# Routed pages of a mixture of experts: two accumulators in place of three, the first twelve pages asked for together, and the experts' splits moved by four pages

## What is computed

```python
x = hidden_states.reshape(-1, H)                  # 2048 tokens, H = 256
topk_w, topk_idx = top_k(softmax(x @ gate_w.T), 4)   # 4 of 16 experts a token
topk_w = topk_w / topk_w.sum(axis=-1, keepdims=True)
shared = (silu(gate) * up) @ shared_down.T        # width 704, every token
shared = shared * sigmoid(x @ shared_gate_vec.T)
for each expert e:                                # inner width 176
    h = silu(x @ w_gate[e].T) * (x @ w_up[e].T)
    acc = acc + (h @ w_down[e].T) * weight_of_e[:, None]
out = x + layernorm(shared + acc)
```

## Time and profile before

| | before |
|---|---|
| time, median of 3 runs | 621.13 us (619.58 to 626.93) |
| the profiled execution's own time | 622.44 us |
| its span, first to last instruction | 620.7 us |
| mean granted TensorE clock | 0.938 |
| instructions | 11606 |
| DMA | 86.34 MB, mean 139 GB/s |
| PE / DVE / ACT / POOL busy | 84 / 66 / 55 / 53% |

### The profile page before, as it was taken

One profiled execution on the slowest core, in us unless ns is written; L12 is line 12 of the kernel. 1 busy time (PEld: TensorE's weight loads), 2 busy tenths in 40 slices (PEclk: granted clock), 3 DMA queues, 4 the chain that ended last, 5 costly groups with the idle time before them and its releaser, 6 DMA issues.

```text
span 620.7 us, 11606 instructions
## 1 busy us (share of the span) xinstructions
PE 523.1 (84%) x3550; PEld 401.6 (65%) x3550; DVE 408.0 (66%) x1005; ACT 342.7 (55%) x701; POOL 325.9 (53%) x357
## 2 busy tenths in 40 slices
PE   2737899899999998878887886968999999999573
PEld 1624455656565453356666775857999999999452
DVE  6539878888788857249735644635997666665337
ACT  2241576696578558655442315535887666666314
POOL 5431543481464215215276566624778887777624
PEclk9859899999999999989897988987999999999878
DMA  7231661535063440340036323439998888887595
GB/s 271 74 129 52 194 192 46 168 128 155 21 216 104 132 136 2 101 141 2 9 138 214 119 81 123 164 125 256 230 248 164 147 150 141 138 134 108 68 343 199
DMA packets 71034, 86.34 MB, mean 139 GB/s; under 512 B 6272, under 2 KB 64192, under 8 KB 70976
## 3 DMA queue, kind: packets, MB, share of 16 engines
q1 hardware_dynamic: 53264, 63.15, 32.3%
q0 software_dynamic: 14448, 19.31, 18.0%
q10 hardware_dynamic: 3264, 3.15, 1.5%
HBM read 33.68 MB, written 39.12 MB: 117 GB/s over the span
## 4 chain that ended last, share of the span: by engine, by line
PE 35%; DVE 8%; issue 4%; DMA 3%; ACT 3%; another core or an unknown queue 2%; POOL 1%; ACTq 0%; POOLq 0%; SPq 0%; DVEq 0%
PE gate_ps L1953 12%; PE y_ps L1976 7%; PE y_ps L1929 3%; PE m_ps L1871 3%; PE gate_ps L939 2%; PE up_ps L939 2%; PE up_ps L1964 1%; PE up_ps L1965 1%; DVE hid L1677 1%; PE gate_ps L1985 1%; DVE hid_lo L1707 1%; ACT yst L1393 1%; DMA added<-acc_dram 1%; PE up_ps L1985 1%
## 5 line engine op out<-in xcount | busy, mean ns | idle before, releaser
L1288 POOL DMA_INDIRECT acc_dram<-yout,xin x79 | 125.5, 1588 | 54.4 <-ACT yout L1421 26.7
L703 DVE TENSOR_REDUCE nmax<-a_ps 128x2 f32<-128x768 f32 (+3 forms) x88 | 96.0, 1119 | 13.7 <-PE a_ps L838 13.2
L588 ACT ACTIVATE probs<-a_ps 128x1024 f32<-128x1024 f32 (+1 forms) x96 | 81.3, 883 | 29.2 <-PE a_ps L860 25.2
L489 POOL TENSOR_SCALAR_AFFINE_SELECT probs<-probs 128x256 f32<-128x256 f32 (+1 forms) x96 | 47.1, 501 | 92.3 <-ACT probs L588 92.2
L1276 POOL DMA_INDIRECT xs_dram<-xrow,idx x64 | 66.3, 1037 | 43.4 <-issue 27.0
L1953 PE MATMUL gate_ps<-w_all,rxT_hi 128*128 x316 | 78.2, 330 | 1.6 <-issue 0.9
L1755 DVE TENSOR_TENSOR h<-rsilu,gate_ps 128x176 f32<-128x176 f32 x79 | 26.6, 337 | 51.8 <-ACT rsilu L1406 40.9
L1976 PE MATMUL y_ps<-w_all,hT_hi 128*128 x237 | 58.0, 313 | 0.3 <-DVE hT_lo L1762 0.2
L1953 PEld LDWEIGHTS gate_ps<-w_all,rxT_hi 128*128 128x128 f32 x316 | 53.0, 192 | 3.2 <-issue 3.0
L833 PE MATMUL a_ps<-KTt,QT 96*128 96x128 bf16 (+3 forms) x256 | 50.3, 307 | 4.6 <-DVE nmax L703 2.2
L860 PE MATMUL a_ps<-QT,KTt 99*128 99x512 bf16 (+3 forms) x256 | 47.8, 301 | 4.7 <-DMA QT<-nT 1.8
(11 more groups left out here) (315 smaller groups left out, 1372.0 us busy)
## 6 DMA issues: line engine op xcount, KB each, us to landing
xin<-xs_dram SPq DMA_DIRECT2D x79, 136.5 KB
xs_dram<-zeros SPq DMA_DIRECT2D x7, 1365.0 KB, 6.6
w_all<-in_wex_dram SPq DMA_DIRECT2D x16, 480.0 KB
QT<-parts SPq DMA_DIRECT2D x48, 128.0 KB
KTt<-parts SPq DMA_DIRECT2D x48, 128.0 KB
acc_dram<-zeros SPq DMA_DIRECT2D x6, 640.0 KB, 8.1
added<-acc_dram ACTq DMA_DIRECT2D x12, 256.0 KB, 9.3
x_all<-in_x_dram SPq DMA_DIRECT2D x4, 512.0 KB, 7.3
```

Source lines behind the costliest of these rows:

```text
L489: pool.affine_select(out=pr, in_=pr, pattern=[[0, nh], [1, P]], compare_op=ALU.is_ge, fill=0.0, base=0, channel_multiplier=-1).then_inc(ma ...
L588: nc.scalar.activation(dst, src, ACT.Exp, scale=float(DH) ** -0.5).then_inc(a_act, 1)
L703: nc.vector.tensor_reduce(nmax[:, i, h:h + nh].rearrange("p (b h) -> p b h", h=hb), src, AX.X, ALU.max, negate=True).then_inc(a_dve, 1)
L1288: pool.indirect_dma_start(out=acc[a][:, :], out_offset=bass.IndirectOffsetOnAxis(ap=xin[:, p % XIN, XROW - 1:XROW].bitcast(mybir.dt.uint32 ...
```

## The change

ACCS goes from 3 to 2: POOL's adds alternate between two accumulators, page p waits for page p-2, the third accumulator isn't allocated, zeroed or loaded (ZEROS 17 to 13, 24 to 16 loads in the tail), and the tail sums two parts. SP asks for pages 0 to 11 in a row, then stores the last part of the shared result, then loads three experts, and from page 16 on one expert behind every second page. The experts' splits on ACT and DVE in the page loop come SPLIT = 4 pages later. PE's transposes of pages 0 and 1 and ACT's roundings of them stand behind the shared expert's last step instead of inside it.

```diff
-XIN, YOUT, ACCS = 12, 6, 3
+XIN, YOUT, ACCS = 12, 6, 2
-ZPAGES, ZACC, ZEROS = 10, 5, 17
+SPLIT = 4
+ZPAGES, ZACC, ZEROS = 10, 5, 13
...
-                half = t["acc"][1 + j // 4]
-                tiles = slice(j % 4 * ZACC * P, min(NT + 1, (j % 4 + 1) * ZACC) * P)
-                for to, n in ((t["xs"][rows, :], XROW), (half[tiles, :], D)):
+                places = [(t["xs"][rows, :], XROW)]
+                if j < 4:
+                    places.append((t["acc"][1][j * ZACC * P:min(NT + 1, (j + 1) * ZACC) * P, :], D))
+                for to, n in places:
...
-            for q in range(PAGES):
+            def load_page(q):
+
                 if q >= XIN:
                     sp.wait_ge(y_added[(q - XIN) % ACCS], 16 * ((q - XIN) // ACCS + 1))
                 sp.dma_start(xin[:, q % XIN, :], xs[q * P:(q + 1) * P, :]).then_inc(xin_in[q % XIN], 16)
-                if q == 4:
-                    store_shared(B - 1)
-                k = early + (q - 5) // 2
-                if q >= 5 and q % 2 == 1 and k < E:
-                    if k == early:
-                        sp.wait_ge(down_done, NSTEP)
-                        sp.wait_ge(tab_ready, 1)
-                        for i in range(2):
-                            sp.wait_ge(ysh_stored[i], 16 * (B // 2))
+
+            for q in range(XIN):
+                load_page(q)
+            store_shared(B - 1)
+            sp.wait_ge(down_done, NSTEP)
+            sp.wait_ge(tab_ready, 1)
+            for i in range(2):
+                sp.wait_ge(ysh_stored[i], 16 * (B // 2))
+            for k in range(early, early + TAILS):
+                expert(k)
+            for q in range(XIN, PAGES):
+                load_page(q)
+                k = early + TAILS + (q - SPLIT - XIN) // 2
+                if q >= SPLIT + XIN and (q - SPLIT) % 2 == 0 and k < E:
                     expert(k)
...
-                load_sums(sp, h, range(0, ACCS, 2 if h % 2 else 3))
+                load_sums(sp, h, range(0, 1))
...
-                if n == NSTEP - 1:
-                    rows_high(0)
-                    rows_high(1)
...
+            rows_high(0)
+            rows_high(1)
...
-                if p >= 2 and early + (p - 2) // 2 < E:
-                    if p % 2 == 0:
-                        expert_high(early + (p - 2) // 2)
+                k = early + (p - SPLIT - 2) // 2
+                if p >= SPLIT + 2 and k < E:
+                    if (p - SPLIT) % 2 == 0:
+                        expert_high(k)
                     else:
-                        expert_tail_high(early + (p - 2) // 2)
+                        expert_tail_high(k)
...
-                load_sums(act, h, range(1, ACCS - h % 2))
+                load_sums(act, h, range(1, ACCS))
...
-                if n == NSTEP - 1:
-                    turn_in(0)
-                    turn_in(1)
...
+            turn_in(0)
+            turn_in(1)
```

More of the change, by code:

```diff
@@ L1765, in _ @@
                     select(p // 2)
-                if p >= 3 and early + (p - 3) // 2 < E:
-                    if p % 2 == 1:
-                        expert_low(early + (p - 3) // 2)
+                k = early + (p - SPLIT - 3) // 2
+                if p >= SPLIT + 3 and k < E:
+                    if (p - SPLIT) % 2 == 1:
+                        expert_low(k)
                     else:
-                        expert_tail_low(early + (p - 3) // 2)
+                        expert_tail_low(k)
             def half_batch(h):
```

## The result

The changed kernel takes **656.9 us** (median of 6 runs, 656.12 to 660.25) against 620.32 us for the kernel before, measured again beside it (6 runs). The ratio is **1.0571, 95% interval 1.0536 to 1.0607**: slower by 5.7%, on the predicted side and inside the range of 634 to 661, but 11 us above the predicted 646. The profiled execution is the slowest of the six: 660.25 us, with a span of 658.5, against 622.44 and 620.7 before.

The account below looks back on a forecast made before the run. With two accumulators, each add's wait for page p-2's landing was taken to bound the kernel, above PE's and POOL's pace. Pages +28.4 us and tail -3.0 gave +25.4 on the 621.1 us median: 646 us, range 634 to 661.

Parts of the forecast that it names:

- (a): First add, behind twelve page loads and the last shared store: moves from 420.79 to about 420.0 us.
- (b): Pages 0 and 1 add while three experts load: 7.5 us plus 0.8 is 8.3, so page 2 starts at 428.3.
- (c): Page 2's round, in a lull of the expert loads: 4.5 us, so page 4's add starts at 432.8.
- (d): Pages 4 to 20, eight two-page rounds beside eight expert loads: landing 5.0 us, round 5.8, together 46.4 us.
- (e): Pages 20 to 78, 29 two-page rounds: landing 3.85 us plus 0.8, so 4.65 each, together 134.9 us.
- tail: Sums and normalisation after the pages: fewer loads and sums save 3.0 us, with 2 and 6 as ends.
- Rival D: Landings of the adds don't gate; PE's 2.0 us a page decides: 610 us, not slower; chance 0.04.
- Rival C: Slower pace empties the DMA queue; all landings from page 2 on take 3.63 us, rounds 4.43: 629 us; chance 0.09.
- Rival E: PE's clock falls because PE now waits: 0.25 us more over 58 pages, +15, 661 us; chance 0.08.
- Rival B: DMA contention stays as it was: +8 us beside the expert loads, +6 in later pages, 660 us; chance 0.14.
- Edits priced at zero: Expert shift and moved transposes: gains go into slack before POOL's chain; without the chain worth up to about 8 us.

Follow-up runs that it names:

- serial_adds: The changed kernel with each add waiting for the landing of the page just before it, so one add in flight: 823.85 us, ratio 1.3245.
- acc2_only: The kernel before with two accumulators (with the change's zeroing and tail loads) and nothing else changed: ratio 1.0578.
- sp_nops: The changed kernel with 40 empty instructions on SP behind each page load from page 31 on: ratio 1.0593.
- more_fetch: The changed kernel with 12 empty instructions a page on PE and 12 on DVE from page 20 on: ratio 1.0609.
- no_page_loads: The changed kernel without the loads of pages 12 to 78, which use the rows of the first twelve again: ratio 1.0488.

## Why the prediction came out as it did

The steps of the sum against the trace of the change (us; SP's store of the shared result, then POOL's adds of pages 0, 1, 2, 4 and 20; the add of page 78 is in the chain row above):

```profile
414.36 0.43 SPq L1185 DMA_DIRECT2D acc_dram<-yst  x1
...
421.95 1.59 POOL L1296 DMA_INDIRECT acc_dram<-yout,xin  x1 [15.05 <-DMA acc_dram<-yst]
423.84 1.58 POOL L1296 DMA_INDIRECT acc_dram<-yout,xin  x1 [0.31 <-issue]
429.65 1.54 POOL L1296 DMA_INDIRECT acc_dram<-yout,xin  x1 [4.23 <-DMA acc_dram<-yout,xin]
...
435.07 2.34 POOL L1296 DMA_INDIRECT acc_dram<-yout,xin  x1 [1.79 <-ACT yout L1428]
...
485.14 1.54 POOL L1296 DMA_INDIRECT acc_dram<-yout,xin  x1 [3.19 <-DMA acc_dram<-yout,xin]
```

| step | predicted | measured | off by |
|---|---|---|---|
| (a) first add | 420.0 | 421.95 | +1.9 |
| (b) pages 0 to 2 | 8.3 | 7.70 | -0.6 |
| (c) pages 2 to 4 | 4.5 | 5.42 | +0.9 |
| (d) pages 4 to 20, eight rounds | 46.4 (5.8 each) | 50.1 (6.26) | +3.7 |
| (e) pages 20 to 78, 29 rounds | 134.9 (4.65 each) | 143.0 (4.93) | +8.1 |
| last landing | 3.63 | 3.77 | +0.1 |
| tail | -3.0 | -4.8 | -1.8 |
| span | 646.1 | 658.5 | +12.4 |

**The mechanism was right.** Rival D (landings don't gate) falls with serial_adds, and with acc2_only, where nothing but the number of accumulators and its consequences is changed. The prediction's own sign of error, two adds to one accumulator less than 4.4 us apart, doesn't occur: the shortest distance in the trace is 4.51 us. PE's 17 of 20 us and the first statistics 5.6 us after the last landing (5.5 forecast) came as said; POOL's waits came to 74.8 us, above the 40 to 60. Rival C (adds land at the minimum) falls: 4.93 a round, not 4.43. Rival E (PE's clock falls) falls too, though not because the clock never fell in the page loop. The windows of its stretches at half rate, and of the late pages, are (columns as before):

```profile
448.50:451.90 3.40, 3.40 (x16) 3.33 (x15) 2.18 (x8) 0.66 (x2) 2.00 (x2) 0.50 0.96 248
...
486.10:489.40 3.30, 3.30 (x16) 3.23 (x14) 2.32 (x8) 0.80 (x3) 2.12 (x2) 0.50 0.82 213
...
500.00:615.70 115.70, 101.54 (x714) 93.26 (x713) 61.10 (x237) 60.69 (x189) 72.17 (x47) 1.00 0.67 107
615.80:639.60 23.80, 4.30 (x10) 2.96 (x10) 1.43 (x5) 0.68 (x2) 10.23 (x9) 0.50 0.62 130
```

Beside the expert loads the clock was at half rate (1.2 of 2.4 GHz) twice, after PE had stood still for 3.63 us (up to 447.27) and for 1.26 us (up to 485.01). Neither cost time, because the outputs that POOL adds there were ready 7 us and more ahead. In the late pages, where E was to cost its 15 us, the clock is 1.00 with PE busy 88% of the time (101.54 of 115.70 us), and it falls only when the pages end. By the Trainium skill's "TensorE: Matmul & The Clock Gate", section "Part 1: The HAM clock gate (the "warmup" mystery)", activity releases the half rate, and the trace agrees here: in both short stretches PE was busy throughout, and the clock came back.

**Rival B comes nearest in size.** Its 660 us is 3 us from the measured 656.9, and my 646 is 11 from it. Page 20's add starts at 485.14, which I had named as B's sign (485 or more). In this trace a round beside the expert loads took 6.26 us, between my 5.8 and B's 6.8, and (e) was at B's 4.85 and a little over. So adds do land later than I took, and the forecast holds in its range rather than in its number.

**The term that was mis-sized is (e),** two thirds of the miss: 4.65 us a round against 4.93. I took the quiet landing, 3.71, and added 0.15 for long ones, from one row. Three accumulators hide long landings from POOL (its 11.0 us of waits), but on a chain every one of them counts in full. Their mean could have been read from the trace of before: the 27 late adds all of whose semaphore updates it has land 3.94 us after their start, where I took 3.85. That is 2.6 us of the 8.1. In the change the same reading gives 4.05 (26 even pages), another 3.2 us; a few adds that start later than the release make up most of the rest. Measured with one add in flight (serial_adds) a landing and its release take 4.61 us, and 4.65 was right for that. Two adds in flight with page loads beside them make it 4.93; the page loads explain the median (4.78 to 4.60), not the mean. The other kernels with two accumulators and page loads have 4.92 to 5.00, so this part of the miss is no accident of one trace.

**(d)** was sized by a choice of 5.0 us between 3.71 and 7.72, on the ground that fewer adds in flight are faster. It was 5.44 in this trace, which is that of the slowest of the six runs. The same instructions gave rounds of 5.95 and 5.85 us in sp_nops and more_fetch, close to the 5.8 of the sum, so most of the 3.7 us in this row may belong to this execution. Without page loads the round was 5.28, 0.6 to 1.0 us less, so page loads are part of what lengthens the adds there.

**(a)** had the start of the store right (415 us; it was issued at 414.36) and its length wrong: I took the 2.92 us of before, but page 0's add, which waits for it, starts at 421.95, and with the release of 0.81 taken off that makes 6.8 us from issue to landing. So the first add moved back (it had been at 420.79) instead of forward. That the twelve loads ahead of the store slow it is likely, and no run varied it.

**The tail** gave 4.8, not 3.0. From the last landing to the second half-batch's statistics it is now 8.65 us (631.90 to 640.55), where it was 11.3: 2.6 us less, of which I had priced 1.2. From there to the last statistics it is 11.0 us where it was 13.1: 2.1 less, priced at 1.8. So the mis-sized term is the start of the tail. The first half-batch's statistics alone came 2.3 us sooner, and the second's stand behind them: I should not have taken less for the second than the 1.7 us that I had worked out for the first.

**Edits priced at zero.** Right with two accumulators: acc2_only and the change have the same ratio. The reason given, slack behind the store and the landings, holds: PE is full from 420 to 435 us and its outputs were later ready some 9.5 us ahead of POOL's use. But "without the chain worth up to 8 us" was wrong: with three accumulators the whole order costs 3 us. Part of the reason is that the experts now come late, since the version that asks for them earlier gains 3 us instead. The 3.6 us that I allowed ACT to stand for one expert was 4.5 at most, 21.6 us in all, hidden as said.

## What to carry to other kernels

Where a resource is held from issue to landing, its cost is (landing + release) divided by the number of them, and it becomes the bound when this passes the pace of the others: here (3.7 + 0.8) / 3 = 1.5 us a page sat under PE's 2.0, and 4.93 / 2 = 2.5 stands above it. When that happens, price the term by the mean of the landings with their long ones, not by the common one, since the slack that hid them is gone. A wait that the profile names after the last engine to finish may belong to the transfer that released both: compare when the named output was ready with when it was used.

## What the runs showed of the hardware

An indirect add of 128 rows of 1 KB to DRAM takes about 3.7 us from POOL's start (1.54 us of it on POOL) to its landing when little else moves. The mean of the late adds is 3.75 us with one in flight (serial_adds), 4.05 with two (the change, even pages) and 3.94 with three accumulators (before). I had not expected one add more or less in flight to change the single landing so little. Beside the expert loads of the change it was 4.1 to 6.2 us. From a landing to the next add on a waiting POOL it was 0.81 us. With three accumulators the landings cost POOL 11.0 us of waiting in all. Program fetches (16 KB, about 1 us on one DMA engine) fall in most of the longest rounds of no_page_loads and go with rounds 0.39 us longer over six traces; whether they cause them was not settled.
